# A four-layer transformer kernel: values' products in pairs, full-array work in the slots between, normalised inputs turned one step sooner

## What is computed

```python
def _L0_ffn_ref(x, ln1_w, ln1_b, ln2_w, ln2_b, w_qkv, b_qkv, w_o, b_o, w_gate, w1, b1, w2, b2):
    ...
    def attention(x, w_qkv, b_qkv, w_o, b_o):
        ...
        scores = jnp.einsum('bqhd,bkhd->bhqk', q, k) / jnp.sqrt(jnp.float32(dh)).astype(x.dtype)
        probs = jax.nn.softmax(scores, axis=-1)
        ctx = jnp.einsum('bhqk,bkhd->bqhd', probs, v).reshape(B, T, D)
        return ctx @ w_o + b_o
    ...
    h = x + attention(layer_norm(x, ln1_w, ln1_b), w_qkv, b_qkv, w_o, b_o)
    return h + moe_ff(layer_norm(h, ln2_w, ln2_b), w_gate, w1, b1, w2, b2)
x = L0_attn_a_x
x = x + _L0_attn_a_ref(_layernorm(x, axis=-1), L0_attn_a_Wq, ...)
x = x + _L0_ffn_ref(_layernorm(x, axis=-1), L0_ffn_ln1_w, ...)
x = x + _L0_attn_b_ref(_layernorm(x, axis=-1), L0_attn_b_Wq, ...)
x = x + _L0_ffn_ref(_layernorm(x, axis=-1), L0_ffn_ln1_w, ...)
```

## Time and profile before

| | before |
|---|---|
| median of 3 runs | 901.11 us (899.53 to 1022.9) |
| span of the profiled execution | 896.4 us |
| TensorE matmul busy | 767.0 us (86%) |
| VectorE busy | 544.5 us (61%) |
| ScalarE busy | 543.4 us (61%) |
| GpSimd busy | 484.2 us (54%) |
| mean granted TensorE clock | 0.923 of full speed |

### The profile page before, as it was taken

The page is one execution under the profiler, slowest core; times in us unless marked ns, Lnnn a source line. Parts: engine busy times, 40 slices in busy tenths (PEclk is TensorE's granted clock), DMA queues, the critical chain, the costliest instruction groups (busy, mean ns, idle before and its releaser), DMA issues.

```text
span 896.4 us, 21301 instructions
## 1 busy us (share of the span) xinstructions
PE 767.0 (86%) x7166; PEld 546.7 (61%) x7166; DVE 544.5 (61%) x1370; ACT 543.4 (61%) x1264; POOL 484.2 (54%) x906
## 2 busy tenths in 40 slices
PE   1999999999999399697988999999999948968970
PEld 1756655666565189497964565566666525958970
DVE  4699899788988123012486887878889822211232
ACT  0377777878787256154546676787877834715640
POOL 6667678747762621504645665844777273060436
PEclk9999999999999789698999899999999977978995
DMA  9300000000000436266210000000000042635842
GB/s 274 111 3 3 3 2 3 4 3 3 4 2 4 130 107 175 79 182 175 79 38 13 16 18 5 4 3 3 3 3 3 3 124 77 173 103 143 245 124 67
DMA packets 57657, 56.29 MB, mean 63 GB/s; under 512 B 6856, under 2 KB 42448, under 8 KB 57552
## 3 DMA queue, kind: packets, MB, share of 16 engines
q1 hardware_dynamic: 39200, 39.13, 15.5%
q0 software_dynamic: 4096, 8.40, 3.2%
q10 hardware_dynamic: 14256, 7.41, 2.9%
HBM read 40.10 MB, written 14.29 MB: 61 GB/s over the span
## 4 chain that ended last, share of the span: by engine, by line
PE 56%; DVE 21%; issue 11%; POOL 7%; DMA 3%; ACT 2%; another core or an unknown queue 0%; ACTq 0%; POOLq 0%; DVEq 0%; SPq 0%
DVE M L1109 11%; PE bankO L466 11%; PE bankR L720 8%; PE bankE L707 7%; PE bankE L485 7%; PE bankE L439 6%; DVE QKV L1071 2%; POOL Yg L1578 2%; PE bankR L452 2%; PE bankE L476 2%; PE bankR L506 2%; PE bankR L536 1%; PE bankR L738 1%; PE bankR L554 1%; DMA Yg<-sorted_y,SLOT 1%
## 5 line engine op out<-in xcount | busy, mean ns | idle before, releaser
L1109 DVE TENSOR_REDUCE M<-bankR 128x2 f32<-128x512 f32 x512 | 326.4, 684 | 62.7 <-PE bankR L452 56.9
L834 ACT ACTIVATE Pr<-bankE 128x512 f32<-128x512 f32 x512 | 277.7, 595 | 129.5 <-PE bankE L439 109.1
L466 PE MATMUL bankO<-Pr,Vx 128*32 128x256 f32 x2048 | 170.5, 406 | 18.8 <-issue 16.1
L452 PE MATMUL bankR<-KQ 32*128 32x256 f32 x1024 | 171.3, 339 | 5.0 <-DVE M L1109 2.9
L439 PEld LDWEIGHTS bankE<-KQ 32*128 32x128 f32 x1024 | 79.6, 188 | 97.1 <-issue 64.2
L439 PE MATMUL bankE<-KQ 32*128 32x256 f32 x1024 | 133.3, 335 | 0.5 <-issue 0.5
L1312 DVE COPY Yb<-bankR 128x128 f32<-128x128 f32 x92 | 26.4, 290 | 167.9 <-PE bankR L720 111.1
L452 PEld LDWEIGHTS bankR<-KQ 32*128 32x128 f32 x1024 | 110.1, 191 | 17.1 <-DVE M L1109 12.8
L951 ACT ACTIVATE G<-bankE,W 128x128 f32<-128x128 f32 x368 | 101.5, 384 | 24.8 <-PE bankE L707 14.0
L707 PE MATMUL bankE<-XTT,W 128*128 128x128 f32 x736 | 105.1, 288 | 11.4 <-issue 4.6
L1578 POOL DMA_INDIRECT Yg<-sorted_y,SLOT x64 | 62.2, 971 | 95.6 <-DMA sorted_y<-Yb 42.0
(11 more groups left out here) (169 smaller groups left out, 1147.0 us busy)
## 6 DMA issues: line engine op xcount, KB each, us to landing
W<-in_w1b SPq DMA_DIRECT2D x92, 258.0 KB
sorted_y<-Yb ACTq DMA_DIRECT2D x92, 64.0 KB
XT<-sorted_u SPq DMA_DIRECT2D x20, 256.0 KB
sorted_u<-Yg SPq DMA_DIRECT2D x2, 1472.0 KB, 9.7
KQ<-MT SPq DMA_DIRECT2D x128, 4.0 KB
X<-in_x SPq DMA_DIRECT2D x8, 128.0 KB, 7.3
sorted_u<-U,SLOT POOLq DMA_INDIRECT x64
Yg<-sorted_y,SLOT POOLq DMA_INDIRECT x64
```

The costliest lines, as they stand in the source:

```text
L452: k = mm(dve_bank("raw", layer, b, h)[:, z * T:z * T + T], QT[rows, kb, g, z * P:z * P + P], KT[rows, kb, g, :], start=True, stop=True)
L466: k = mm(bankO[SL * j:SL * j + SL, cols], Vx[:, b % VB, kc, HG * g + j, :], Pr[:, g % 2, j, kc, :], start=(g % 2 == 0 and kc == 0), stop=( ...
L834: nc.scalar.activation(Pr[:, (h // HG) % 2, h % HG], act_bank("S", layer, b, h).rearrange("p (k q) -> p k q", k=TT), ACT.Exp, scale=EXP_SC ...
L1109: v.tensor_reduce(M[:, b % 2, :, h], dve_bank("raw", layer, b, h).rearrange("p (t k) -> p t k", t=TT), AX.X, ALU.max, negate=True).then_in ...
```

## The change

In TensorE's step the two halves of a group's products with values (kc 0 and 1) are issued one behind the other, in slots 0, 2, 4 and 6. Full-array work stands in slots 1, 3, 5 and 7. For rope and ffn blocks zT is issued at the end of the step before the one that projects (for block `p` instead of `n`), and GpSimd's `norm` of such a block always comes first in its step. Covariance blocks keep zT in slot 0. kT is in slot 5 and qT in slot 7 for every layer (rope had them in 6 and 7). zT waits for 8, 14 or 8 of the counts of `z_ready` instead of 9, 15 or 8. ScalarE and VectorE follow with the order of their copies.

```diff
+        Z_READY = {"rope": 8, "ffn": 14, "cov": 8}
...
+        def turned_ahead(q):
+
+            return LAYERS[q[0]] != "cov"
...
             def do_zT(layer, b):
-                need(pe, z_ready, layer, b)
+                need(pe, z_ready, layer, b, Z_READY[LAYERS[layer]])
...
             def step(u, t, a, m, n, p):
+
                 if a:
                     do_scores(*a, 0)
                     do_raw(*a, 7)
-                if n:
+                if n and not turned_ahead(n):
                     do_zT(*n)
                 if t:
                     do_pv(*t, 3, 0)
+                    do_pv(*t, 3, 1)
...
-                if t:
-                    do_pv(*t, 3, 1)
                 if n:
                     do_proj(*n)
...
                 if a:
                     do_pv(*a, 0, 0)
+                    do_pv(*a, 0, 1)
...
-                if a:
-                    do_pv(*a, 0, 1)
+                if u:
+                    do_uT(*u)
...
-                if u:
-                    do_uT(*u)
                 if a:
                     do_pv(*a, 1, 0)
+                    do_pv(*a, 1, 1)
...
-                if n and LAYERS[n[0]] != "rope":
+                if n:
                     do_kT(*n)
-                if a:
-                    do_pv(*a, 1, 1)
-
+                if u:
+                    do_gate(*u)
                 if m:
                     do_mT(*m, 0)
+                if t:
+                    do_onT(*t)
+
...
                 if a:
                     do_pv(*a, 2, 0)
+                    do_pv(*a, 2, 1)
...
                     do_raw(*m, 6)
+                if n:
+                    do_qT(*n)
                 if t:
                     do_wo(*t)
-                if n and LAYERS[n[0]] == "rope":
-                    do_qT(*n)
-                if a:
-                    do_pv(*a, 2, 1)
+                if p and turned_ahead(p):
+                    do_zT(*p)
...
             def step(u, t, a, m, n, p):
-                early = (t and LAYERS[t[0]] == "rope") or (n and LAYERS[n[0]] == "rope") or (3, 0) in (n, p)
+                early = p and turned_ahead(p)
```

More of the change, by code:

```diff
@@ L885, in step @@
                     do_exp(*a, 0)
-                if n:
+                if n and not turned_ahead(n):
                     do_zT(*n)
+                if t:
+                    do_pv(*t, 1)
                 if a:
@@ L899, in step @@
                 if a:
+                    do_exp(*a, 4)
                     do_exp(*a, 5)
-                if n and LAYERS[n[0]] != "rope":
+                if n:
                     do_kT(*n)
```

31 lines of the change are left out of this document (6 added, 25 removed).

## The result

| | before | after |
|---|---|---|
| median, us | 900.75 (899.53 to 1022.9, 4 runs) | 887.33 (886.43 to 888.12, 4 runs) |
| profiled execution, span us | 896.4 | 885.4 |
| TensorE busy, us | 767.0 | 740.4 |
| VectorE, ScalarE, GpSimd busy, us | 544.5, 543.4, 484.2 | 539.2, 533.9, 482.5 |

The ratio is 0.9869, with a 95% interval of 0.9843 to 0.9894: the changed kernel is 1.3% faster. One run of the kernel before, the one of 1022.9 us, was a slow one, and the ratio is of fast runs alone. 887.33 lies inside 884 to 911, but the forecast was 896, 5 us of gain, and the gain is 12 us by the ratio and 13 by the medians.

A forecast was written before the change was run, and what follows sets the result against it. The prediction took TensorE and VectorE to hand the step's end to each other, so TensorE savings pay only where VectorE waits. Gains of 3 + 1.6 + 0 + 0 + 0.7, about 5, took 901.1 to 896 us; range 884 to 911.

The forecast's parts named there:

- ffn with gating: Ffn steps with gating: a later raw product 5 offsets a shorter end; 16.1 us a step as now, 0 gained.
- The beginning of that step: From the projection's addition to raw product 5, with gate and onT now ahead of it: 8.55 us instead of 7.97.
- third rival: Scores of slot 6 wait for ScalarE to free four full banks; from 0.6 us a step, 2% slower; chance 0.10.
- Rope: Rope steps: 10.74 us unchanged plus 5.27 on TensorE make 16.0 against 16.44; 0.4 gained, times 8 is 3.
- ffn without gating: Ffn steps without gating: 15.3 us for 15.52 now; 0.2 gained, times eight is 1.6.
- Covariance: Covariance steps: gain before the projection met by later raw products; 0, between -0.2 and +0.2 us a step.
- Start: First zT, no longer waiting for the normalisation's last addition, starts about 0.7 us earlier.
- The price of a switch: Leaving a TensorE tiling mode costs 0.09 us, taken the same for full-array work.
- Second PV call: Second of two back-to-back PV calls on TensorE: 0.48 us taken, bounds 0.36 and 0.57.
- All switches land: Rival: at most 256 dropped TensorE mode switches at 0.09 us all pay, 23 us, giving 877; chance 0.13.
- bankE runs full: Rival: kT, mT and onT fill four banks in slot 5, scores wait for ScalarE; 922 at 0.8 a step; chance 0.10.
- the chain: Step picture: only TensorE's path to raw product 5, VectorE's chain, and the path from last maximum to addition count.

The follow-up runs named there:

- e4: Kernel before with only GpSimd's order of the changed kernel, the next block's normalisation first in rope and ffn steps: 899.13 us.
- e11: Changed kernel with GpSimd normalising the next block last in steps with gating, behind the stacked queries and values: 894.48 us.
- e3: Changed kernel with zT back in slot 0 of its own step for all layers: 896.66 us.
- e5: Changed kernel with gate moved from slot 5 to slot 7 and VectorE's copy of the gate values behind maxima 6: 894.93 us.
- e1_pairs: Kernel before with only the two PV calls of a group put in one slot (0, 2, 4, 6): 915.41 us against 899.29.
- e7: Changed kernel with two ffn moves, kT from slot 5 to slot 3 and qT from slot 7 to slot 5, and later normalisation in gating steps: 906.21 us.

## Why the prediction was wrong, point by point

- **ffn with gating**: the step of the prediction that failed, 4.2 us where it had 0. Its sum for a step was 8.55 + 2.87 + 2.26 + 1.29 + 1.15 = 16.12. In the last such step of a layer it measured 8.65 (raw product 5, 234.25 to 242.90) + 2.22 (to 245.12) + 2.26 (to 247.38) + 2.37 (to the addition at 249.75) = 15.50. **The mis-sized term is the 2.87 of maxima 5, gate copy and weights, from raw product 5 to the next maxima. It measured 2.22 there, 2.13 in the step ahead and 1.49 in the first, which has no weights at all.** The prediction read the term off one step as work of VectorE that the change leaves alone, and used it for all steps with gating.

The three steps of the first ffn layer, in us, each from addition to addition:

| step with gating | to raw 5 | raw 5 to the next maxima | to the last four maxima | to the addition | sum |
|---|---|---|---|---|---|
| first, before | 7.97 | 2.71 | 2.27 | 3.10 | 16.05 |
| first, after | 8.66 | 1.49 | 2.58 | 2.51 | 15.24 |
| second (choice), before | 7.96 | 2.83 | 2.26 | 3.09 | 16.14 |
| second, after | 8.66 | 2.13 | 2.26 | 2.37 | 15.42 |
| last (weights), before | 7.97 | 2.87 | 2.26 | 3.08 | 16.18 |
| last, after | 8.65 | 2.22 | 2.26 | 2.37 | 15.50 |

VectorE behind raw product 5 in the first of them, before and after:

```profile
219.40 1.29 DVE L1109 TENSOR_REDUCE M<-bankR 128x2 f32<-128x512 f32 x2 [0.52 <-PE bankR L452]
...
222.11 1.29 DVE L1109 TENSOR_REDUCE M<-bankR 128x2 f32<-128x512 f32 x2 [1.34 <-PE bankR L452]
```

```profile
212.25 1.29 DVE L1103 TENSOR_REDUCE M<-bankR 128x2 f32<-128x512 f32 x2 [0.65 <-PE bankR L457]
213.74 1.29 DVE L1103 TENSOR_REDUCE M<-bankR 128x2 f32<-128x512 f32 x2 [0.20 <-PE bankR L457]
```

Two things set the term, and whichever ends last counts. One is TensorE. In the old order raw product 6 comes 2.71 after raw product 5 (this step, and all three of e4), in the new one it can come after 1.49, since qT no longer stands between them. The other is VectorE's own work. In the last step it went from 2.87 to 2.22: 0.08 is the gate copy, which the prediction itself had moved ahead of maxima 5 and still counted here. The other 0.57 is weight operations that no longer stand beside a busy GpSimd, since the change moves GpSimd's normalisation out of that place. e4 shows that the shortening alone is worth 0.1 in the old order, which holds the step at 2.71. e11 shows that giving the overlap back costs 0.9 in the new one. e3 shows that the end of the step is as short only with zT a step sooner. That the sooner raw product 6 is what the first step gains is read from its rows; no run changes it by itself.

- **The beginning of that step**: right in size, 8.65 for 8.55, wrong in its reason, and so partly luck. Gate ahead of raw 5 was charged at 0.46; e5 shows 0, since the scores of slot 6 stand until ScalarE has emptied the banks of kT. This is the third rival in a small form. Two of the signs that the prediction named came out otherwise: VectorE's wait for raw 5 is 1.02, not above 1.13, since VectorE itself comes later to it; and a step below 15.7 was to mean that raw 5 isn't late, but it is late.
- **How many steps**: ten were counted with gating, five of each layer. Only three of each have a projection to be timed by. The others run in the drain, and the stretches with it show no gain.
- **Rope**: right in its sum. From the end of the stacked queries to the addition it is 5.31 us, predicted 5.27, and full-clock steps are 16.01 for 16.43 (predicted 16.0), others 15.75 for 16.43 and 16.65 for 16.85. The parts offset each other: wo takes 0.42 instead of 0.56 and mT 0.14 instead of 0.22, but the addition waits for VectorE's last two maxima (75.33 to 76.53), which the prediction had not put on the path. The other two of the five rope steps gave 3 us more, part of it by less half clock. Three of the eight steps are filling, and show no gain.
- **ffn without gating**: 15.23 to 15.36, predicted 15.3; 2.5 us in eight steps instead of 1.6. Whether the way there was the predicted one was not followed row by row.
- **Covariance** 0: right, -0.5 with a scatter of 1.8 between two executions of one kernel.
- **Start** 0.7: gained between two instructions, not visible in the whole.
- **The price of a switch**: 0.09 was taken for every kind. Behind the output projection it is 0.17 (e3).
- **Second PV call**: 0.43, inside its bounds of 0.36 and 0.57 and 0.05 below the 0.48 taken.
- **All switches land**: no, and e1_pairs contradicts it most plainly. **bankE runs full**: the waits ahead of slot 6 and in it are 0.5 at most in ffn steps.

The direction and the range held; the range was wide for the unknown price of a second PV call, and that price is not what moved the time. As a theory that could be carried to another order, the chain failed at once (e1: 885 to 889 expected, 915 measured).

The profiles differ by 10.0 us on average and the medians by 13. The prediction put 4.7 us between the profile's span and the time of a run. Every run whose span was taken has 1.8 between them, so the profiled executions of the kernel before were faster ones, of 898.2 and 895.24 us where the median is 900.75, and those of the changed kernel, of 887.2 and 886.21, stand near its median. What stays open is what the slower executions spend their time on, and why the stretch ahead of the experts is longer in the changed kernel.

## What to carry to other kernels

Where one engine feeds another through a few banks, look at how far apart the products come, and not only at how much work or how many mode switches the feeder has. An uneven order of less work lost 15 us, and one transposition moved from a long slot to a short one gave 14 back. But adding up slot lengths is no forecast: the next move by the same sum lost 25 us (e7). A term read off one step holds for that step: where two engines meet, write down what each of them needs, and take the later one again in the new order and in every kind of step. When a change moves one engine's work, also take the operations of the engines that work beside it as changed, and ask whether the time they free has something waiting behind it: the same overlap was worth 0.1 us in one order and 0.9 in another. Test the parts of such a change together too, since here each of two halves loses and the whole gains.

## What the runs showed of the hardware

- Two PV calls back to back take 16 matmuls in 1.07 us, against 0.64 for one, so the second costs 0.43.
- An output projection of four full-array matmuls takes 0.42 us to the next start when full-array work follows, and 0.59 when row-tiled scores follow.
- A VectorE operation of 4 to 32 elements a partition with both inputs in SBUF took 0.16 to 0.20 us beside an idle GpSimd, and 0.51 to 0.70 when one of GpSimd's operations of 0.75 ran, ending within 0.1 us of it.
- Behind waits of TensorE of 2.3 and 4.4 us the granted clock was 0.53 and 0.50 for 1.8 us and more (PV pair 1.87 instead of 1.07). In rope and covariance steps it falls in another step from one execution to the next.
